# Five small tensors moved behind the last large buffer in a 16-head attention and feed-forward kernel: only SBUF addresses differ

## The reference

```python
x = L0_attn_x                                   # (1, 2048, 256)
xn = _layernorm(x, axis=-1)
# attention: 16 heads of 128, S = 2048
qkv = einsum('bsd,ed->bse', xn, Wqkv)
w = softmax(einsum('bqhd,bkhd->bhqk', q, k) * 128 ** -0.5)
attn = einsum('bse,de->bsd', einsum('bhqk,bkhd->bqhd', w, v), Wout)
# feed-forward with ternary weights, 256 -> 704 -> 256
ffn = _bitlinear(sigmoid(_bitlinear(xn, w1)) * _bitlinear(xn, w2), w3)
return x + attn + ffn
```

## Time and profile before

| | us |
|---|---|
| median of 3 runs | 1910.93 |
| lowest and highest of them | 1906.85, 1912.75 |
| profiled execution, its own time | 1910.57 |
| its span, first to last instruction | 1908.7 |

### The profile page before, as it was taken

How to read it: one execution, slowest core, us unless ns; L and a number is a source line. 1 busy time by engine, 2 the same in 40 slices (tenths; PEclk the granted TensorE clock), 3 DMA queues, 4 the chain that set the end, 5 groups by cost and what they waited for, 6 DMA issues and landing times.

```text
span 1908.7 us, 33423 instructions
## 1 busy us (share of the span) xinstructions
PE 1862.1 (98%) x11588; PEld 1665.3 (87%) x11588; DVE 1594.4 (84%) x2088; ACT 1252.2 (66%) x1700; POOL 1347.9 (71%) x514
## 2 busy tenths in 40 slices
PE   5989999999999999999999999999999999999998
PEld 4868888898888989888888988888898988889887
DVE  6368888888888889888888988888898888888885
ACT  4337676666767666666767667676766667676665
POOL 2418687776868777686877768687776868776685
PEclk9999999999999999999999999999999999999999
DMA  3037677676767767676776767677676767767664
GB/s 106 0 74 177 160 168 170 153 175 156 175 159 170 172 153 172 160 173 156 175 171 154 171 160 172 158 175 171 154 171 160 169 161 171 175 147 171 156 159 128
DMA packets 195830, 298.65 MB, mean 156 GB/s; under 512 B 37888, under 2 KB 57024, under 8 KB 195776
## 3 DMA queue, kind: packets, MB, share of 16 engines
q1 hardware_dynamic: 195776, 298.01, 66.7%
HBM read 12.65 MB, written 2.10 MB: 8 GB/s over the span
## 4 chain that ended last, share of the span: by engine, by line
PE 79%; POOL 6%; SPq 5%; issue 4%; DVE 3%; ACT 1%; DMA 1%; POOLq 0%; DVEq 0%; ACTq 0%
PE ps_o L371 30%; PE ps_s L362 10%; PE ps_s L363 10%; PE ps_s L364 10%; SPq L279 5%; POOL parts L1035 4%; PE ps_t L352 4%; PE ps_s L333 4%; PE ps_t L342 4%; PE ps_s L405 2%; PE ps_o L380 1%; PE ps_o L382 1%; PE ps_o L381 1%; DVE prob L891 1%; DMA raw<-prob 1%
## 5 line engine op out<-in xcount | busy, mean ns | idle before, releaser
L1035 POOL TENSOR_TENSOR parts<-raw,parts 128x2048 fp32r<-128x2048 f32 x254 | 1175.7, 4629 | 443.6 <-ACT parts L669 443.5
L681 ACT ACTIVATE prob<-ps_s,neg_max 128x1024 f32<-128x1024 f32 x512 | 567.0, 1114 | 449.0 <-DVE neg_max L885 448.8
L881 DVE TENSOR_REDUCE row_max<-ps_s 128x1 f32<-128x1024 f32 x512 | 613.0, 1213 | 114.1 <-PE ps_s L364 95.7
L891 DVE STREAM_TRANSPOSE prob<-prob 128x1024 f32<-128x1024 f32 x508 | 599.5, 1218 | 60.7 <-ACT prob L681 60.3
L669 ACT CAST parts<-raw 128x2048 fp32r<-128x2048 f32 x254 | 486.3, 1915 | 105.8 <-DMA raw<-prob 104.3
L371 PE MATMUL ps_o<-parts,v_hi 128*128 128x256 f32 x4064 | 515.8, 280 | 4.8 <-POOL v_lo L1028 4.8
L371 PEld LDWEIGHTS ps_o<-parts,v_hi 128*128 128x128 f32 x4064 | 497.9, 189 | 20.5 <-POOL v_lo L1028 6.1
L362 PE MATMUL ps_s<-k_hi,q_hi 128*128 128x512 f32 x1024 | 402.6, 393 | 12.5 <-ACT prob L681 11.5
L363 PE MATMUL ps_s<-k_lo,q_hi 128*128 128x512 f32 x1024 | 400.3, 391 | 0.0
L364 PE MATMUL ps_s<-k_hi,q_lo 128*128 128x512 f32 x1024 | 400.1, 391 | 0.0
L371 PE MATMUL ps_o<-parts,v_lo 128*128 128x256 f32 x2032 | 275.6, 278 | 0.0
(11 more groups left out here) (111 smaller groups left out, 1571.6 us busy)
## 6 DMA issues: line engine op xcount, KB each, us to landing
raw<-prob SPq DMA_DIRECT2D x2032, 128.0 KB, 2.4
v_raw<-v_turned SPq DMA_DIRECT2D x244, 64.0 KB, 2.0
w_raw<-wqkv_dram SPq DMA_DIRECT2D x32, 128.0 KB, 2.5
y<-x_dram SPq DMA_DIRECT2D x4, 512.0 KB, 6.1
wo_raw<-wqkv_dram SPq DMA_DIRECT2D x16, 128.0 KB, 2.5
wo_raw<-wo_dram SPq DMA_DIRECT2D x16, 128.0 KB, 2.3
out_dram<-y SPq DMA_DIRECT2D x8, 256.0 KB, 2.7
w_raw<-w_dram SPq DMA_DIRECT2D x2, 704.0 KB, 10.6
```

The source lines that it names most:

```text
L681: nc.scalar.activation(tile, logit, ACT.Exp, bias=neg_max[:, t:t + 1], scale=SCALE, accum_out=row_sum[:, t, half:half + 1]).then_inc(s_exp, 1)
L881: nc.vector.reduce_max(row_max[:, t, half:half + 1], ps_s[:, 2 * half:2 * half + 2, :].rearrange("p b n -> p (b n)"), AX_X).then_inc(s_mx, 1)
L891: nc.vector.transpose(tile, tile).then_inc(s_xp, 1)
L1035: nc.gpsimd.tensor_tensor(half_of(0, half), moved(p, half), half_of(1, half), ALU.subtract).then_inc(s_pl, 1)
```

## The change

The five calls that lay out `row_max`, `neg_max`, `row_sum`, `denom` and `inv_denom` stand behind the one for `parts` in place of ahead of the feed-forward tensors. They take 128, 64, 128, 64 and 64 bytes of a partition, 448 together.

```diff
         o_hi = sb("o_hi", [P, 2 * P], F32R)
         o_lo = sb("o_lo", [P, 2 * P], F32R)
-        row_max = sb("row_max", [P, T, 2])
-        neg_max = sb("neg_max", [P, T])
-        row_sum = sb("row_sum", [P, T, 2])
-        denom = sb("denom", [P, T])
-        inv_denom = sb("inv_denom", [P, T])
 
         with ExitStack() as early:
...
         parts = sb("parts", [P, T, 2, 8, BLK], F32R)
+        row_max = sb("row_max", [P, T, 2])
+        neg_max = sb("neg_max", [P, T])
+        row_sum = sb("row_sum", [P, T, 2])
+        denom = sb("denom", [P, T])
+        inv_denom = sb("inv_denom", [P, T])
```

## The result

The changed kernel takes 1930.89 us (1929.61 to 1932.33, 5 runs) against 1910.93: 1.0106 times as long, 95% interval 1.0095 to 1.0117. The prediction was 1910.9 us and no change, with a range of 1904 to 1917. It is 20.0 us slower, outside the range.

The account below looks back on a forecast made before the run. PE's matmul count times cadence was taken to bound the kernel. All terms were 0, so the profiled 1910.57 us stayed; the forecast was the three runs' median, 1910.9 us, no change, range 1904 to 1917.

Parts of the forecast that it names:

- What bounds the kernel: Twelve of sixteen heads: PE busy 1330.36 of 1331.00 us, so time is its matmul count times their cadence.
- PE on `parts`: 6096 product matmuls in 254 steps reading `parts`: 0 us taken, with ends -1.3 and +7.6.
- this trace holds both placements: Pricing of each engine: moved tensors at 64, unmoved at 128, so a pair of rows gives the price.
- Stands next to a step and not where it reads: Product steps: the pair's 0.03 us put down to neighbours, since two steps at one address differ by 0.10 us.
- ACT, POOL, DVE: 0 us: Instructions on moved tensors, 1915, 4629 and 717 ns: no change; POOL's end +0.20 us a step.
- Transfers: 0 us: Transfers from `prob` into `raw` and `v_raw`: no change by the rows; the 256-byte rule would give +1.1 us.
- The small tensors: 0 us: One to 32 elements at a time on DVE, ACT, POOL: same place modulo 256, fixed cost, 0 us.
- Rival 1: Product matmuls: PE streams the moved operand faster, 46 us gained, 1865 us; chance 3%.
- the slower rivals: Slower writes into `raw`, +9.6 us, 1920 us, chance 5%; POOL's low parts 0.20 us longer, 1917 us, chance 2%.
- What would show it: Changed profile: L371's 24 matmuls still 2.73 and 2.83 us, ACT, POOL, DVE within 1%, landing 2.4 us, `v_lo` waits 5 us.
- both signs that were named for "wrong": L371's 24 matmuls below 2.7 us, or PE waits for `v_lo` or `parts` each head with landings above 2.7 us.

Follow-up runs that it names:

- e8: Moving operands in the heads (xt, k, wo, parts) 64 past a multiple of 256, stationary ones 128, small tensors filling gaps: 1925.43 us, 1.0076 of the kernel before.
- e15: `q_hi`, `q_lo` moved to 192 modulo 256, `k` at 128, `parts` at 64 as in the kernel before: 1921.59 us, 1.0063 of the kernel before.
- e3: Changed kernel with `v_hi`, `v_lo` and `parts` all moved by 64 bytes, to 192 modulo 256: 1929.62 us, 1.0102 of the kernel before.
- e4: Changed kernel with `v_hi` and `v_lo` moved by 64 bytes to 192 modulo 256, `parts` left at 128: 1917.19 us, 1.0039 of the kernel before.
- e11: `parts` and `wo` at 64 modulo 256, all other operands of TensorE at 128: 1912.84 us, 1.0020 of the kernel before.
- e2: Changed kernel with `prob` and `raw` moved by 64 bytes to 192 modulo 256, `parts` at 0: 1930.8 us, 1.0106 of the kernel before.
- e6: Changed kernel with 192 unused bytes ahead of `parts` alone, putting it back at 64 modulo 256: 1909.29 us, 0.9995 of the kernel before.
- e5: Large tensors at the kernel before's addresses (`inv_denom` and 384 unused bytes ahead), four small tensors behind `parts`: 1911.08 us, 1.0004 of the kernel before.
- e14: Changed kernel with `v_lo` alone moved by 64 bytes, to 192 modulo 256: 1926.28 us, 1.0083 of the kernel before.
- e7: Changed kernel with `parts` 32 bytes later, at 160 modulo 256, `v_hi` and `v_lo` at 128: 1917.17 us, 1.0040 of the kernel before.
- e9: Changed kernel with a gap of 224 bytes ahead of `parts`, putting it at 96 modulo 256: 1920.96 us, 1.0063 of the kernel before.
- e10: Changed kernel with a gap of 160 bytes ahead of `parts`, putting it at 32 modulo 256: 1920.59 us, 1.0059 of the kernel before.
- e1: Changed kernel with 64 unused bytes between `raw` and `parts`, putting `parts` at 192 modulo 256: 1920.95 us, 1.0059 of the kernel before.

## Why the prediction was wrong, point by point

- **What bounds the kernel** held. PE's cadence is the time, and nothing on another engine showed. For that very reason the 2 to 6 ns that a product matmul got longer (from 114 or 118 to 120) could not be hidden anywhere.
- **The step that failed is "PE on `parts`"**, "I take 0, with -1.3 and +7.6 as ends". It had the right row and read it against the wrong one. The last pair's products read `xt_hi` at 128 against `v_hi` at 128, which is the relation that the change gives `parts`, and take 2.86 us. I set this against 2.83, the slower of the two kinds of step, and put the rest down to neighbours. The steps on `parts` alternate, so the fair partner was their mean, 2.78: 254 x 0.08 = 20.3 us. The runs showed 2.87 and 2.88 for every kind of step, and the change costs 20.0. That the two sums come this near is in part luck: the steps on `parts` grew by 0.095 us, not 0.08, and the kinds of step and their neighbours make up the difference. The other partner, 24 matmuls of 512 columns at 5.45 us, was no partner: e8 and e15 show that 512 columns answer with the opposite sign.
- **The assumption under it**, that each tensor's own place is what may count ("this trace holds both placements"), was wrong by e3 and e4. What counts most is the pair of operands of a matmul. I compared `parts` at 64 with other tensors at 128 without asking where their stationary partners were.
- **"Stands next to a step and not where it reads"** was half right. The neighbours have a part in which steps take 2.73 and which 2.83 (e11), though e8 has both forms behind the same neighbours. But this alternation is itself part of the placement: at the new place it is gone.
- **ACT, POOL, DVE: 0 us** held: 1915, 4635 and 715 ns.
- **Transfers: 0 us** held (e2, e6). The rule of the Trainium skill that was weighed ("DMA: Bandwidth & Descriptors", "How a descriptor splits into AXI transactions") gives 3% more beats at 128 than at 64. The trace doesn't bear it out: the landing took 2.3 us against 2.4, and the packets took 66.1% of 1930.5 us, 1276 us, where they took 66.7% of 1908.7, 1273.
- **The small tensors: 0 us** held (e5 for four of them, e6 for all five).
- **Rival 1** named the right mechanism's neighbourhood, a cadence that depends on where `parts` starts, with the wrong sign and 3%. A rival "the cadence of L371 rises" with the 2.86 us row, and with its own chance, was missing; the slower rivals were given to transfers and POOL.
- **What would show it**: both signs that were named for "wrong" failed to appear. The sign that did, 24 matmuls above 2.83 us, wasn't on the list.

Shown: the cause is the place of `parts` against `v_hi` and `v_lo` (e3, e4, e6, e14). Argued only: that the matmul's stream and the load of a coming matmul's weights meet in the same part of the memory. The loads overlap the streams. The loads of `v_hi` and `v_lo` (PEld, L371) got longer with the change, from 189 and 188 ns to 192 each, and those of the logits' weights stayed at 188 to 189; in e14 the loads of `v_lo` take 190. But with 512 columns the streams got longer and the loads did not (188 ns in e15), and no run took a load away. Open: the map from places to cadence (e7, e9, e10 and the fourth pair, e4), and what puts a step into its 2.73 or its 2.83 us form (e8, e11).

## What to carry to other kernels

When PE is busy all the time, an edit of addresses alone can move the time by 1%. In this kernel the moving operand of the 256-column fp32r matmuls is best 64 bytes below the stationary one's place, every equal place modulo 128 that was tried was slowest, and the 512-column ones are better even. This is a map of one kernel and no rule: seven expectations that applied such a rule to a new place or tensor missed in size or sign (e1, e4, e7 to e11). Before taking such a term as 0, price it by a pair of rows of the same shape in which both operands' places are known, against the mean of all forms that the group takes, and check the alternation of steps. Freeze the large tensors' addresses (a gap of the same size) when small tensors are moved around.

## What the runs showed of the hardware that was not expected

- The cadence of back-to-back 256-column fp32r matmuls takes a few values that hold for a whole step: in the kernels before and after 24 of them take 2.73, 2.83 or 2.88 us, 114, 118 or 120 ns each, and other placements give values between (2.80 in e7, 2.84 in e9). It does so at the same granted clock, 1.00, and with no wait in the profile; PE is shown as busy in all of them.
- The sign depends on the size: 64 bytes below gains 2 to 6 ns at 256 columns (120 to 118 or 114), and costs about 6 ns at 512 (5.59 against 5.45 us for 24).
- At one and the same addresses a step takes one of two cadences, and it can keep it for ten steps (e8: 2.72 and 2.73 us, then 2.83).
- With `prob` and `raw` at a place of 192 (e2) the transfer engines' packets took 69.3% of 1929.1 us, 1337 us, where 64 and 128 gave 1273 and 1276. The landing stayed at 2.4 us and the time at that of the changed kernel, so it was free here; three places in one kernel don't make a rule.
